# A bound and a masked index list for the last pass of row gathers in a four-layer graph network

## The chip, the cores and the metric

The kernel runs on one core of one Trainium2 chip. The metric is the device time of one execution in microseconds, the median of several runs. A profile is one execution recorded by the hardware profiler; its span runs from the first to the last recorded instruction.

## The reference, cut to what matters

The graph has 6250 nodes of 256 features and 106250 edges, sorted by the node they end in (`dst`). Four layers follow each other. Each normalises the node rows, multiplies them by weights, and sums over each node's incoming edges a weighted copy of the source node's row. In the first layer the weight is a hyperbolic distance factor, in the second and third a softmax-like score, and in the last layer, the one this change is about, there is none:

```python
summed = segment_sum(feat[src], dst, num_segments=n)
deg = segment_sum(ones_like(dst), dst, num_segments=n)
h_neigh = (summed / maximum(deg, 1.0)[:, None]) @ w_neigh.T
rst = feat @ w_self.T + b_self + h_neigh      # x = x + rst
```

## The kernel before, in words

**Tiles and steps.** The 6250 nodes are 49 blocks of 128 (`NB`), the 106250 edges are 831 tiles of 128 (`ET`). Edges are sorted by target, so a tile's edges end in one block, or, where a tile crosses from one block to the next, in two. The work on edges goes in steps. A step is one tile together with one block; a tile that crosses a border is taken twice, once for each block. That gives 831 + 48 = 879 real steps (`S_REAL`), padded to `S` = 880. In `dst_tab` each edge of a step has the number of its target inside the step's block; a number below 0 or above 127 means that the edge belongs to the neighbouring block. `src_tab` holds the source node's number, as an int32. Slots of the last tile and of the last step that hold no edge have source 0 and a target far away.

**A pass over the edges.** Each layer stores its 49 blocks of transformed rows in a table in HBM (6272 rows of 259 float32: 256 features and three extra columns). Then it runs over the 880 steps:

- GpSimd (POOL) gathers, with one indirect DMA for a step, the 128 source rows of the step's edges from the table into a slot of the ring (`ring`, 40 slots, which lies over the tile `X`). In `gathers(q)` (q = 0, 1, 2 for the second to the fourth layer) it waits before every fifth gather until the five slots have been read (semaphore `used`).
- VectorE (DVE) compares 0 to 127 with `dst_tab` and so makes the one-hot matrix of the step. In the last layer `ones` does so for five steps at a time (line 1129). An edge outside the block gets a row of zeros.
- TensorE (PE) multiplies the one-hot matrix with the gathered rows (line 585, `sum_step`). Both blocks' steps of a crossing tile gather the same 128 rows, and the zeros make sure that each edge counts once.
- DVE adds the product to the block's running sum (`add_sum`, line 1142).

**Between the passes** of the third and the fourth layer DVE finishes the last blocks' ELU (`weighed` and `elu`, lines 1670 and 1675) beside ScalarE (ACT, `elu_parts`), then `norm_pipe(3, ...)` adds to X and normalises, PE multiplies by the weights, and SyncE (SP) stores the table. `gathers(2)` begins when all seven parts of the table are stored and X has been saved.

**In the last pass** PE also multiplies each block by `w_self` every 17 steps (lines 560, 567 and 568), and DVE adds `add_mean` (line 1720) in the last 49 steps; then SP stores the result.

**Memory that the change reuses.** `plain` is a scratch tile of 16 x 128 bfloat16 for each partition. In the third pass `dst_rows` lies in it. `not_own` is the tile `w_tab`; the second layer reads it last.

Of the kernel before, what the change touches and what calls it, by code (L numbers as in the profile page):

```python
# [13 lines left out]
P = 128  # L14
F32 = mybir.dt.float32
BF16 = mybir.dt.bfloat16
I32 = mybir.dt.int32
ALU = mybir.AluOpType
# [4 lines left out]
NB = -(-N // P)  # L23
# [9 lines left out]
S = ITERS * RING  # L33
# [8 lines left out]
SLOTS = 40  # L42
# [3 lines left out]
BATCH = 5  # L46
# [30 lines left out]
def gnn_program(nc, x, src, dst, edge_weight, w0, bias0, w1, b1, mag_w, mag_b, attn_w, w2, a2,  # L77
                w_neigh, w_self, b_self, out):
    with ExitStack() as ctx:
        def sb(name, shape, dt=F32):  # L80
            return ctx.enter_context(nc.sbuf_tensor(name, shape, dt))
# [3 lines left out]
        def sem(name):  # L85
            if name not in sems:
                sems[name] = ctx.enter_context(nc.semaphore(name))
            return sems[name]
# [7 lines left out]
        plain = sb("plain", [P, RING, P], BF16)  # L96
        src_tab = sb("src_tab", [P, S], I32)
        dst_tab = sb("dst_tab", [P, S])
# [33 lines left out]
        table = nc.dram_tensor("table", [NB * P, W], F32, kind="Internal").ap()  # L132
# [29 lines left out]
        ring = x_flat[:, 0:SLOTS * W].rearrange("p (k w) -> p k w", k=SLOTS)  # L162
# [19 lines left out]
        hots = onehot[:, 0:HOTS, :]  # L182
        spare = onehot[:, HOTS:, :].rearrange("p k e -> p (k e)")
        plain_flat = plain[:, :, :].rearrange("p k e -> p (k e)")
        dst_rows = plain_flat[:, 0:2 * BATCH * P].rearrange("p (m k e) -> p m k e", m=2, k=BATCH)
        hot_t = spare[:, 0:BATCH * P].bitcast(BF16).rearrange("p (m k e) -> p m k e", m=2, k=BATCH)
        no_link = plain_flat[0:1, 0:CW]
# [5 lines left out]
        not_own = w_tab[:, :]  # L193
# [261 lines left out]
        @block.gpsimd  # L455
        def _(pool):
            pool.iota(iota_i, [[1, S]], base=0, channel_multiplier=0).then_inc(sem("iotas"), 1)
            pool.iota(tno_i, [[P, EC]], base=0, channel_multiplier=1).then_inc(sem("iotas"), 1)
            pool.memset(ident[:, :], 0.0).then_inc(sem("ident_zero"), 1)
            pool.wait_ge(sem("ident_zero"), 1)  # L460
            pool.affine_select(out=ident[:, :], in_=ident[:, :], compare_op=ALU.not_equal, fill=1.0, base=0,
                               pattern=[[-1, P]], channel_multiplier=1).then_inc(sem("iotas"), 1)

            def gathers_layer0():
                for s in range(S):
                    if s % LAND == 0 and s >= SLOTS0:
                        pool.wait_ge(sem("used"), SLOTS + s + LAND - SLOTS0)
                    pool.indirect_dma_start(ring0[:, s % SLOTS0, :], None, table,  # L468
                                            bass.IndirectOffsetOnAxis(src_tab[:, s:s + 1], 0)
                                            ).then_inc(sem(f"batch0_{s // LAND % (SLOTS0 // LAND)}"), 16)  # L470

            def gathers(q):
                pool.wait_ge(sem("x_kept"), 16 * OUTER * (q + 1))
                for s in range(S):
                    if s % BATCH == 0:

                        pool.wait_ge(sem("used"), (q + 1) * S + s + BATCH)
                    pool.indirect_dma_start(ring[:, s % SLOTS, :], None, table,  # L478
                                            bass.IndirectOffsetOnAxis(src_tab[:, s:s + 1], 0)
                                            ).then_inc(sem(f"batch_in{s // BATCH % (SLOTS // BATCH)}"), 16)  # L480

            pool.wait_ge(sem("steps_out"), 16 * (2 * EC + 2))
            pool.memset(A[:, :, :], 0.0).then_inc(sem("sums_zero"), 1)
            pool.wait_ge(sem("table_stored"), 16 * OUTER)
            gathers_layer0()
            for q in range(3):
                pool.wait_ge(sem("table_stored"), 16 * OUTER * (q + 2))
                gathers(q)
# [507 lines left out]
        def _(dve):  # L996
            chain = Chain(dve, "vec_step")
            ts, tt, stt = dve.tensor_scalar, dve.tensor_tensor, dve.scalar_tensor_tensor
# [33 lines left out]
            for c in range(EC):  # L1032
                ins = dve.memset(parts_of["tile"][0][:, c, :], float(P * c))
# [11 lines left out]
            for c in range(EC):  # L1045
                ins = ts(pick[:, c, :], iota_s, t_start[:, c:c + 1], None, ALU.is_ge)
            chain(ins)
            for c in range(EC):
                ins = stt(pick[:, c, :], iota_s, t_end[:, c:c + 1], pick[:, c, :], ALU.is_le, ALU.mult)
            ins.then_inc(sem("tiles_picked"), 1)  # L1050
            dve.wait_ge(sem("weights_turned"), 1)
            for n, name in enumerate(("w0T", "w1T", "wnT", "wsT")):
                ins = dve.tensor_copy(wT[name][:, :, 0:D], psum[:, 4 + n, :].rearrange("p (c d) -> p c d", c=2))
# [9 lines left out]
            for b in range(NB):  # L1063
                ins = dve.bn_stats(out=stats[:, b, 0:6], in_=X[:, b, :])
# [32 lines left out]
            for c in range(EC):  # L1097
                n = min(P, S - c * P)
                ins = dve.tensor_copy(turned_dst[0:n, c, :], psum[0:n, c // 4, c % 4 * P:c % 4 * P + P])
            for h in range(2):  # L1100
                a, z = h * SH, h * SH + SH
                ins = tt(row_b[:, a:z], row_a[:, a:z], dst_tab[0:1, a:z], ALU.subtract)
            chain(ins)
            for h in range(2):
                a, z = h * SH, h * SH + SH
                ins = tt(row_b[:, a:z], row_b[:, a:z], psum[0:1, 2 + h, 0:SH], ALU.add)
# [11 lines left out]
            for c in range(EC):  # L1118
                n = min(P, S - c * P)
                dve.tensor_copy(rows_out[0:n, c, :], turned_dst[0:n, c, :])  # L1120
                ins = tt(cuts_out[0:n, c, 1:P], turned_dst[0:n, c, 1:P], turned_dst[0:n, c, 0:P - 1], ALU.not_equal)
# [50 lines left out]
            def rows(source, k_scale, b):  # L1172
                return ts(blk(source, b), blk(source, b), colb(k_scale, b), None, ALU.mult)
# [491 lines left out]
            def weight_2(b):  # L1665
                dve.reciprocal(col("t1")[:, b:b + 1], A[:, b, AUX:AUX + 1]).then_inc(sem("weights_2"), 1)
# [10 lines left out]
            def scored_sums():  # L1677
                chain(ts(tiny[:, 7:8], iota_part[:, :], float(TAIL), None, ALU.is_ge))
                chain(dve.tensor_copy(iota_psum, iota_node[:, :]))
                for first in range(SUBS):  # L1680
                    turned_hots(0, first)
                equals(1, 0, 0)
                equals(1, 0, CMP)
                leaky_exponents(0, 0)

                def turn(i, last):
                    for h in range(2):
                        at = blocks_at(mybir.EngineType.DVE, i * SLOTS + h * GR, GR)
                        for k in range(GR):
                            add_sum(1, i, h * GR + k, at[k])  # L1690
                            done = i * SLOTS + h * GR + k - ET
                            if 0 <= done < NB - 1:
                                weight_2(done)
                            if done >= 10:
                                weighed(done - 10)
                            if done >= 11:
                                elu(done - 11)
                            if last and h:
                                continue
                            if k in (0, 4, 8, 12):  # L1700
                                turned_hots(i, SUBS + h * SUBS + k // 4)
                            if k == 2:
                                equals(1, i, (h + 1) * GR)
                            if k == 15:
                                leaky_exponents(i, h + 1)
                            if k == 17:
                                equals(1, i, (h + 1) * GR + CMP)

                for i in range(TURNS):
                    turn(i, i == TURNS - 1)  # L1710
                dve.wait_ge(sem("sum_added"), ACC_BANKS + 3 * S)
# [72 lines left out]
            for c in range(OUTER):  # L1784
                if c < BY_DVE:
                    for b in part(c):
                        ins = rows(H, "t1", b)
# [44 lines left out]
            split_u()  # L1832
            scored_sums()

            chain(tt(A[:, NB - 1, AUX:AUX + 1], A[:, NB - 1, AUX:AUX + 1], tiny[:, 7:8], ALU.subtract))
            weight_2(NB - 1)
            dve.wait_ge(sem("weights_2"), NB)
# [39 lines left out]
```

## Time and profile before

| what | value |
|---|---|
| runs of the kernel before (3) | median 5928.48 us, 5926.69 to 5933.43 |
| span of the profiled execution | 5110.8 us |
| median of the runs less that span | 817.7 us |
| instructions recorded | 58785 |
| POOL busy | 3349.8 us (66% of the span) |
| DVE busy | 3431.6 us (67%) |
| PE busy | 3290.4 us (64%) |
| ACT busy | 1841.1 us (36%) |
| last pass's first to last gather | 3991.37 to 5091.0 us |

The profiled execution's own time outside its span is not recorded: of it only the span is known. The 817.7 us are the difference to the runs, and no record of the trace lies in them. In the rows below "PE", "DVE" and so on are engines, L478 is line 478 of the kernel, an arrow points from what an instruction reads to what it writes, and "idle before" is the time for which the engine stood still just ahead of such instructions, with what ended the wait.

### The profile page before, as it was taken

What the parts mean: (1) busy time and instruction counts of PE and PEld (TensorE: products, weight loads), DVE (VectorE), ACT (ScalarE), POOL (GpSimd) and SP (SyncE); (2) the same over time, 40 slices, a digit from 0 to 9 for tenths busy, and PEclk for the clock granted to TensorE, in tenths of its full rate; (3) what the DMA queues carried; (4) which work ended last, traced back from release to release, by engine and by line L of the source; (5) the groups of instructions that cost most, each with busy time, mean ns of one, the idle gap of its engine ahead of it and who ended that gap; (6) DMA issues with size and microseconds to landing.
All of it is one profiled execution on the core that took longest, in us unless ns stands there. A gap on an engine that the chain in (4) does not pass through costs nothing. (4 is left out here: it accounts for less than half of the span.)

```text
span 5110.8 us, 58785 instructions
## 1 busy us (share of the span) xinstructions
PE 3290.4 (64%) x11755; PEld 2256.4 (44%) x11755; DVE 3431.6 (67%) x10603; ACT 1841.1 (36%) x4370; POOL 3349.8 (66%) x3529
## 2 busy tenths in 40 slices
PE   2788888887444655566655666666666666666666
PEld 1556666655332333333334444444444444444444
DVE  7799999999974666666676555555558455555556
ACT  2455555555782333333344333333337100000000
POOL 1777777774007777777752777777772577777776
PEclk7899999998776777777777888888877877778787
DMA  4444444444024333333445554555554444443434
GB/s 137 136 133 132 134 133 133 133 133 120 11 91 124 107 107 107 107 107 107 107 117 153 132 132 132 132 132 134 133 133 141 138 114 114 114 114 107 113 107 142
DMA packets 302511, 617.15 MB, mean 121 GB/s; under 512 B 66649, under 2 KB 175189, under 8 KB 302166
## 3 DMA queue, kind: packets, MB, share of 16 engines
q0 software_dynamic: 168960, 467.01, 34.5%
q1 hardware_dynamic: 107862, 117.55, 7.5%
q10 hardware_dynamic: 25344, 28.85, 2.0%
q8 instruction: 113, 1.85, 0.1%
q14 instruction: 232, 1.90, 0.1%
HBM read 560.58 MB, written 52.57 MB: 120 GB/s over the span
## 5 line engine op out<-in xcount | busy, mean ns | idle before, releaser
L478 POOL DMA_INDIRECT X<-table,src_tab x2640 | 2500.7, 947 | 1360.5 <-issue 752.1
L585 PE MATMUL psum<-X,onehot 128*128 128x259 f32 x5280 | 1847.6, 494 | 905.8 <-ACT onehot L722 333.6
L1142 DVE SCALAR_TENSOR_TENSOR A<-A,same_tab,psum 128x259 f32 x3476 | 1671.8, 481 | 756.9 <-PE psum L585 531.8
L585 PEld LDWEIGHTS psum<-X,onehot 128*128 128x128 f32 x5280 | 1169.2, 241 | 1376.9 <-ACT onehot L722 582.4
L468 POOL DMA_INDIRECT X<-table,src_tab x880 | 836.9, 951 | 280.7 <-issue 251.6
L722 ACT ACTIVATE onehot<-G,zero_col,ecols 128x128 f32<-128x128 bf16 x1760 | 730.0, 481 | 688.9 <-PE psum L585 451.3
L594 PE MATMUL psum<-H,G 128*128 x1760 | 603.1, 429 | 249.6 <-DVE G L1238 196.3
L574 PE MATMUL psum<-X,onehot 128*128 128x259 f32 x1760 | 567.6, 407 | 4.2 <-ACT onehot L722 2.2
L594 PEld LDWEIGHTS psum<-H,G 128*128 128x128 f32 x1760 | 323.7, 205 | 429.0 <-issue 392.1
L722 ACT ACTIVATE onehot<-onehot,zero_col,coef 128x128 f32<-128x128 bf16 x880 | 365.9, 481 | 128.7 <-DVE coef L1281 103.1
L1238 DVE SCALAR_TENSOR_TENSOR G<-psum,X 128x257 f32<-128x257 f32 x880 | 367.1, 418 | 61.8 <-DMA X<-table,src_tab 38.0
L722 ACT ACTIVATE ecols<-ecols,zero_col 128x20 f32<-128x20 f32 (+2 forms) x187 | 52.4, 302 | 987.5 <-DVE ecols L1663 486.9
L574 PEld LDWEIGHTS psum<-X,onehot 128*128 128x128 f32 x1760 | 357.5, 204 | 71.3 <-issue 10.7
L992 ACT COPY onehot<-psum 128x256 f32<-128x256 f32 x49 | 18.2, 372 | 1020.0 <-PE psum L560 1020.0
L1129 DVE TENSOR_TENSOR G<-psum,dst_tab 128x1280 bf16<-128x1280 f32 x176 | 261.3, 1485 | 34.6 <-ACT onehot L722 34.5
L1245 DVE TENSOR_SCALAR onehot<-iota_b,dst_tab 128x128 bf16<-128x128 bf16 x880 | 230.0, 261 | 0.0
L623 PE MATMUL psum<-ident,ecols 128*20 128x128 f32 x44 | 17.0, 387 | 308.5 <-DVE ecols L1539 308.5
L1657 DVE TENSOR_REDUCE ecols<-psum 128x20 f32<-128x60 f32 x44 | 9.7, 221 | 292.0 <-DMA X<-table,src_tab 292.0
L722 ACT ACT_TABLE_LOAD x137 | 175.8, 1283 | 77.5 <-DVE mv L1072 61.3
L1538 DVE TENSOR_TENSOR ecols<-X,w_tab 128x20 f32<-128x20 f32 x44 | 8.2, 186 | 264.3 <-DMA X<-table,src_tab 264.3
L1129 DVE TENSOR_TENSOR onehot<-psum,dst_tab 128x640 f32<-128x640 f32 x176 | 144.1, 819 | 43.6 <-issue 33.4
L616 PE MATMUL psum<-wide_rows,onehot 128*128 x880 | 131.6, 237 | 58.0 <-issue 38.4
(347 smaller groups left out, 2826.0 us busy)
## 6 DMA issues: line engine op xcount, KB each, us to landing
X<-table,src_tab POOLq DMA_INDIRECT x3520, 2.8
plain<-rows_dram SPq DMA_DIRECT2D x110, 256.0 KB
plain<-rows_dram ACTq DMA_DIRECT2D x176, 160.0 KB, 3.4
table<-H SPq DMA_DIRECT2D x21, 906.5 KB, 8.5
x_dram<-X SPq DMA_DIRECT2D x21, 896.0 KB, 4.1
X<-x_dram SPq DMA_DIRECT2D x14, 896.0 KB, 5.1
X<-in_x SPq DMA_DIRECT2D x2, 6144.0 KB
table<-A SPq DMA_DIRECT2D x7, 906.5 KB, 7.2
```

Of the source, the lines that this page charges most:

```text
L468: pool.indirect_dma_start(ring0[:, s % SLOTS0, :], None, table, bass.IndirectOffsetOnAxis(src_tab[:, s:s + 1], 0)).then_inc(sem(f"batch0_{ ...
L478: pool.indirect_dma_start(ring[:, s % SLOTS, :], None, table, bass.IndirectOffsetOnAxis(src_tab[:, s:s + 1], 0)).then_inc(sem(f"batch_in{s ...
L574: pe.matmul(psum[:, s % ACC_BANKS, 0:W], hots0[:, s % HOTS0, :], ring0[:, s % SLOTS0, :], start=True, stop=True).then_inc(sem("used"), 1)
L585: pe.matmul(psum[:, k % ACC_BANKS, 0:W], hots[:, k % HOTS, :], ring[:, k, :], start=True, stop=True).then_inc(sem("used"), 1)
L594: pe.matmul(psum[:, 4 + s % 4, 0:D + 1], oht[:, s // B0 % 2, s % B0, :], blk(H, at, 0, D + 1), start=True, stop=True).then_inc(sem("own_ro ...
L616: ins = pe.matmul(psum[:, 4 + h, c * OWN:c * OWN + P], hot_t[:, first % 2, k, :], u_parts[:, bass.ds(vs[k] * OWN, P)], start=True, stop=True)
L722: return act.activation(out_, in_, f, **kw)
L992: act.copy(late_v, late_turned).then_inc(sem("late_kept"), 1)
L1129: return tt(out_, numbers.rearrange("p (o n) -> p o n", o=1).to_broadcast([P, n, P]), dst_tab[:, bass.ds(first, n)].rearrange("p (s o) -> ...
L1142: stt(total, total, same, psum[:, t % ACC_BANKS, 0:W], ALU.mult, ALU.add).then_inc(sem("sum_added"), 1)
L1238: stt(junk0[:, q, k % 2, at:at + D + 1], psum[:, 4 + s % 4, 0:D + 1], 1.0, ring0[:, s % SLOTS0, 0:D + 1], ALU.mult, ALU.mult, accum_out=en ...
L1245: ts(equal0[:, s % GR0, :], iota_b[:, :], dst_tab[:, s:s + 1], None, ALU.is_equal).then_inc(sem("equal_0"), 1)
```

## The change

The last pass of gathers (q = 2) reads its indices from a new list, `near_tab`, and gets a bound. In `near_tab` each edge that lies in the step's block keeps its source number, and each other one has 2 * 49 * 128 = 12544 added, so that it is above the last row of the table (6271). The gather is issued with `bounds_check` 6271 and `oob_is_err=False`: rows whose index is above the bound are left out, and their places in the ring keep what they held. They are multiplied by zero later, as before. DVE builds the list with four operations after the third layer's sums, and POOL waits for it (semaphore `near`) before the last pass. The second and third layers' gathers are issued as before, and so are the first layer's.

```diff
@@ -182,6 +182,7 @@
         plain_flat = plain[:, :, :].rearrange("p k e -> p (k e)")
+        near_tab = plain[:, :, :].bitcast(I32).rearrange("p k e -> p (k e)")[:, 0:S]
@@ -471,13 +472,20 @@
             def gathers(q):
                 pool.wait_ge(sem("x_kept"), 16 * OUTER * (q + 1))
+                if q == 2:
+                    pool.wait_ge(sem("near"), 1)
                 for s in range(S):
                     if s % BATCH == 0:
                         pool.wait_ge(sem("used"), (q + 1) * S + s + BATCH)
-                    pool.indirect_dma_start(ring[:, s % SLOTS, :], None, table,
-                                            bass.IndirectOffsetOnAxis(src_tab[:, s:s + 1], 0)
-                                            ).then_inc(sem(f"batch_in{s // BATCH % (SLOTS // BATCH)}"), 16)
+                    if q < 2:
+                        ins = pool.indirect_dma_start(ring[:, s % SLOTS, :], None, table,
+                                                      bass.IndirectOffsetOnAxis(src_tab[:, s:s + 1], 0))
+                    else:
+                        ins = pool.indirect_dma_start(ring[:, s % SLOTS, :], None, table,
+                                                      bass.IndirectOffsetOnAxis(near_tab[:, s:s + 1], 0),
+                                                      bounds_check=NB * P - 1, oob_is_err=False)
+                    ins.then_inc(sem(f"batch_in{s // BATCH % (SLOTS // BATCH)}"), 16)
@@ -1832,6 +1840,10 @@
             split_u()
             scored_sums()
+            ts(not_own, dst_tab[:, :], P - 0.5, float(2 * NB * P), ALU.is_gt, ALU.mult)
+            chain(ts(near_tab, dst_tab[:, :], 0.0, float(2 * NB * P), ALU.is_lt, ALU.mult))
+            chain(tt(near_tab, near_tab, not_own, ALU.add))
+            tt(near_tab, near_tab, src_tab[:, :], ALU.add).then_inc(sem("near"), 1)
             chain(tt(A[:, NB - 1, AUX:AUX + 1], A[:, NB - 1, AUX:AUX + 1], tiny[:, 7:8], ALU.subtract))
             weight_2(NB - 1)
```

## Rows read from the trace of the kernel before

**Rows 1.** The page's groups: busy us, mean ns, then idle before and its releaser

```profile
L478 POOL DMA_INDIRECT X<-table,src_tab x2640 | 2500.7, 947 | 1360.5 <-issue 752.1
```

**Rows 2.** The source view of line 478 in the last pass, 3990 to 5111 us

```profile
L478 POOL DMA_INDIRECT X<-table,src_tab x880: 942/946/1165, 3991.4 to 5091.0; - x176
its engine sat idle before it (us, times) until:
  issue: 261.4, 858
  DMA table<-A: 119.2, 1
  PE psum L585: 6.4, 21
who waited for it (us, times):
  PE psum L585: 104.2, 29
DMA to landing us min/median/max: 2.7/2.8/5.5
```

**Rows 3.** The timeline of POOL at the last pass's start: start, us, what, idle before

```profile
3991.37 0.94 POOL L478 DMA_INDIRECT X<-table,src_tab  x1 [119.23 <-DMA table<-A]
3992.62 0.94 POOL L478 DMA_INDIRECT X<-table,src_tab  x1 [0.30 <-issue]
...
4002.63 0.94 POOL L478 DMA_INDIRECT X<-table,src_tab  x1 [0.30 <-issue]
4003.88 0.95 POOL L478 DMA_INDIRECT X<-table,src_tab  x1 [0.30 <-PE psum L585]
4005.13 0.95 POOL L478 DMA_INDIRECT X<-table,src_tab  x1 [0.30 <-issue]
```

**Rows 4.** The windows view of the last pass: length, busy by engine, granted clock, DMA share, GB/s

```profile
3991.00:5092.00 1101.00, 719.02 (x2142) 504.41 (x2142) 577.75 (x1140) 18.23 (x49) 832.83 (x880) 0.78 0.42 115
```

**Rows 5.** The DMA view of the same stretch, and of the whole span (queue 0 carries the gathers)

```profile
q0 software_dynamic: 42165, 116.56, 39.2%
```

```profile
q0 software_dynamic: 168960, 467.01, 34.5%
```

**Rows 6.** The groups view of POOL by shape, and of DVE by shape

```profile
L468 POOL DMA_INDIRECT X<-table,src_tab x880 | 836.9, 951 | 280.7 <-issue 251.6 <-PE psum L574 16.1 <-DMA table<-H 13.0
L461 POOL TENSOR_SCALAR_AFFINE_SELECT ident<-ident 128x128 f32<-128x128 f32 x1 | 0.3, 292 | 0.2 <-POOL ident L459 0.2
L1868 POOL MEMSET const-float32-0.0<- 128x1 f32 x1 | 0.1, 98 | 0.2 <-issue 0.2
```

```profile
L1112 DVE TENSOR_TENSOR H<-H 1x880 f32<-1x880 f32 x1 | 1.1, 1064 | 0.0
L1094 DVE TENSOR_SCALAR A<-A 128x880 f32<-128x880 f32 x1 | 0.6, 619 | 0.1
L1090 DVE CAST misc<-A 1x880 int32<-1x880 f32 x1 | 0.6, 608 | 0.0
```

**Rows 7.** The timeline of DVE behind the third pass's sums

```profile
3907.22 0.16 DVE L1666 RECIPROCAL cols<-A 128x1 f32<-128x1 f32 x1
3907.48 0.18 DVE L1838 MEMSET A<- 128x147 f32 x1
3907.70 0.36 DVE L1670 TENSOR_SCALAR A<-A,cols 128x256 f32<-128x256 f32 x1
3907.97 0.42 DVE L1675 SCALAR_TENSOR_TENSOR A<-H,A 128x256 f32<-128x256 f32 x1
3908.30 0.35 DVE L1670 TENSOR_SCALAR A<-A,cols 128x256 f32<-128x256 f32 x1
...
3915.85 0.75 DVE L1847 TENSOR_TENSOR X<-X,A 128x256 f32<-128x256 f32 x2
```

**Rows 8.** The timeline of ACT there

```profile
3914.09 0.58 ACT L722 ACTIVATE H<-A,zero_col,cols 128x256 f32<-128x256 f32 x1
3914.59 0.89 ACT L722 ACTIVATE H<-H,zero_col 128x256 f32<-128x256 f32 x2
```

**Rows 9.** The chain that ended last, from 4400 to 5092 us, by line

```profile
by line: POOL X L478 59.3%; issue 22.8%; PE psum L585 8.9%; DVE A L1142 3.3%; DMA X<-table,src_tab 1.8%; DVE onehot L1129 1.2%; DVEq L266 0.8%; PE psum L567 0.7%; PE psum L568 0.4%; DVEq L1142 0.4%; DVE H L1720 0.4%; PE psum L560 0.2%; DVE 
```

## The prediction

> **What bounds the kernel now.** I read the page's groups first. They show which instruction stands at the head of the passes: the indirect gathers of line 478, 2640 of them in three passes, 947 ns each [rows 1]. Next comes the last pass by itself, since only its 880 gathers are changed. The source view of line 478 shows that they start from 3991.4 to 5091.0 us, and that POOL stands idle between them for 261.4 + 6.4 us in 879 gaps, put down to its own issuing in 858 of them [rows 2]. The timeline shows the same as a beat: a start every 1.25 us, made of 0.94 or 0.95 us of work and 0.30 us of gap, with no gap longer than another [rows 3]. From first to last start that is (5091.0 - 3991.37) / 879 = 1.251 us, 880 times over 1101 us. POOL is thus never held up by a full ring in this pass: what it does for one gather sets the beat.
>
> The windows view says how much room the others have. In the 1101 us PE is busy 719.0, DVE 577.8, ACT 18.2 and the DMA engines 42% [rows 4]. A step costs PE 0.82 us and DVE 0.66 us against a beat of 1.25. The chain of waits agrees: over most of this stretch 59% is gathers and 23% issue, 9% is the matmuls [rows 9]. PE waits for a gather only 29 times, 104.2 us in all [rows 2]; it takes five steps at a time when they have landed, so such a wait is the beat seen from the other side. The reader is to see two things. A change of the beat goes one for one into the time, 880 times, from a slower beat at once, and from a faster one down to PE's 0.82 us. Bytes moved, PE and DVE work are beside the point in this pass.
>
> The runs' median, 5928.5 us, is 817.7 us above the profiled span, 5110.8. No row lies in that difference. I take it as unchanged and add the change of the span to the median.
>
> **How many rows are left out.** 880 steps of 128 are 112640 places. Each of the 106250 edges is in its step's block exactly once. So 6390 places, 5.7%, get an index above the bound: 48 crossing tiles taken twice give 48 x 128 = 6144, the last tile's empty places 118, the padded step 128. They lie in some 98 steps; in the other 782, 89%, every row is gathered as before. That weighs on all that follows: whatever the bound costs is paid 880 times, and what it saves is saved in one gather of nine.
>
> **The change part by part.**
>
> *The wait for `near`.* It is an extra wait at the head of the pass. POOL stands there anyway from the third pass's last gather until the table is stored, 119.23 us [rows 3]; the list is ready near 3911, some 80 us before 3991.37. It costs nothing. Without that cover it would cost what is left of the four operations, under 4 us.
>
> *The four DVE operations.* Two TENSOR_SCALAR over 128 x 880: 619 ns for float32, and writing int32 the nearest row is the CAST at 608 ns. Two TENSOR_TENSOR at 1064 ns, the row of 880 float32 [rows 6]. The sum is 2 x 0.62 + 2 x 1.06 = 3.4 us. They stand ahead of `weight_2` of the last block, which starts at 3907.22, and what is queued behind them on DVE is the last ten blocks' ELU and then `norm_pipe(3)`, whose start, at 3915.85, sets the table store and so the first gather. But DVE isn't what sets the pace of these ten blocks at their end: it begins with 0.60 us for a block (3907.70 to 3908.30) and ends waiting for ACT, whose last exponential runs to 3915.48 [rows 7, 8]. ACT isn't late by it: it needs `weight_2` of the last block, now near 3910.8, for the Relu at 3914.09. Ten blocks at 0.60 from 3911.1 end at 3917.1, where they ended at 3915.85: +1.3 us. Bounds: 0 if the operations overlap more, 3.4 if none of it is taken up. I take 1.4, which all goes into the fill between the passes.
>
> *The bytes.* 6390 rows of 1036 bytes are 6.6 MB of the 116.6 MB that queue 0 moves there [rows 5]. The transfers take 2.8 us from issue to landing and forty slots are in flight ahead of PE [rows 2], so a slightly shorter transfer moves nothing. What I take: 0. Semaphore counts are the same, sixteen for each gather, so nothing waits otherwise.
>
> *The register with the bound.* Each gather now carries a bound, perhaps with an instruction of POOL's queue to set it. The nearest row is the semaphore wait that already stands ahead of every fifth gather: the gap with it is 0.30 us as is the one without [rows 3]. POOL's queue takes such an instruction for nothing, while the gather before it works. I take 0; if it lay in the gap, even 30 ns would be 26 us, and that is counted with the next part.
>
> *The gather itself.* No row of this trace has a gather with a bound, so it is bounded from both sides. Work of a gather is 0.946 us for 128 rows, 7.4 ns a row, if none of it is fixed [rows 2]. Below: rows left out cost nothing and the test is free, then the pass is shorter by 6390 x 7.4 ns = 47 us. Above: the test is a piece of work by itself. POOL's smallest instruction, one element in each of 128 partitions, takes 98 ns; its compare-and-select over 128 x 128 takes 292 ns [rows 6]. A list of 128 indices is one element for each row, so the first is nearer. 880 x 0.098 = 86 us; the other, 880 x 0.292 = 257 us. Between -47 and +86 (far end +257) I take 0: nothing in the rows shows that POOL's time follows anything but the count of gathers. The first layer's 880 gathers write to another ring, with other waits, and take 951 ns against 947 [rows 1, 6].
>
> Here the Trainium skill speaks, in "DMA: Bandwidth & Descriptors". Its section "Anatomy of one DMA" has descriptor generation as a small variable share and says that many descriptors can be emitted before the added cost shows: by this rule a gather with fewer rows is no shorter on POOL, and the sum would be 1.4 us instead of down to -46. Its section "SWDGE vs HWDGE vs iDMA" has these DMAs made by software that computes the descriptors, on a core of GpSimd: by that, one more comparison for each index can cost time, which speaks against the change. No row here has two sizes of gather to decide between them.
>
> **The sum.** 0 (wait) + 1.4 (DVE) + 0 (bytes) + 0 (register) + 0 (gather) = +1.4 us on the span of 5110.8, and 5928.5 + 1.4 = 5930 us on the median.
>
> **The rivals.** Of 5928.5 us 0.2% is 11.9 us; that is about what a measurement can tell from no change.
>
> *Nothing to see (0.40).* The bounded gather keeps its 0.946 us and its 0.30 us gap. For it: the regularity of both under different rings and waits. 5930, and 5917 to 5940 with a few ns either way on each gather.
>
> *The test costs time on POOL (0.36).* It is the one on the slower side. The place is the work of each gather, 0.946 us; the price is 0.098 us for each, 6016 us with the DVE term. It decides from (11.9 - 1.4) / 880 = 12 ns for a gather, a tenth of a ns for each index. For it: it is paid 880 times by the one engine without slack, and software that handles 128 indices in 0.946 us has no compare that is known to be free. Against it: the unbounded gather may test already, and skip nothing.
>
> *Rows left out shorten the gather (0.24).* All of the work follows the rows and the test is free: 5930 - 47 = 5883 us. If half of 0.946 us is fixed, -24 gives 5906. It decides from -13.3 us, or 28% of the work following the rows. For it: the descriptors of 128 rows are the obvious thing to take 0.946 us. Against it: it can happen only in one gather of nine, and any test of over 0.3 ns for an index would eat it whole.
>
> *A rival that changes neither sum:* less traffic would let PE run nearer its own pace. DMA engines are at 42% and PE at 65% of the stretch [rows 4], so it is hidden anyway, and I count it with the first.
>
> **How the numbers follow.** Likeliest: 5930. The low end is the third case in full, 5883. The high end takes in the second case at its nearer bound, 6016, with 4 us for the DVE bound and the runs' spread: 6020. Above it stays what a test nearer to the 292 ns row would make, up to 6187, to which I give 0.12, and below 5883 next to nothing. The likeliest case's own range is 5917 to 5940. Faster by over 0.2%: 0.24; within: 0.40; slower: 0.36.
>
> **What would show it right or wrong.** In the profile after, the source view of the bounded gather in the last pass: median 946 ns and a start every 1.25 us for the first case; near 1040 ns or a gap above 0.30 us in all 880 for the second; for the third a low minimum in about 98 gathers, those at block borders, and the old 946 in the rest. The last pass's first gather should start 1 to 2 us later than 3991.4, and DVE should show four operations of 3.4 us in all ahead of `weight_2`. Queue 0 should move some 6.6 MB less. The prediction is wrong if the beat of the pass moves by more than 12 ns.

## The result, and the profile after

| | median us | runs |
|---|---|---|
| before | 5927.35 | 20, 5918.19 to 5935.75 |
| changed | 5937.6 | 20, 5928.73 to 5951.26 |

The ratio is 1.0019, 95% interval 1.0013 to 1.0025: 11 us slower by the ratio, 10 by the medians, just inside the 11.9 us that count as no change here. Two later sets of runs gave 1.0022, just outside it. The forecast of 5930 in a range of 5883 to 6020 holds, but not by the way it was argued: the bound is not free, and most of its price didn't reach the end.

The first surprise is the page of the changed kernel. Its span is 5937.8 us, as long as its runs. That of the kernel before was 5110.8, 818 us short of them.

```profile
span 5937.8 us, 59670 instructions
PE 3574.5 (60%) x11755; PEld 2297.5 (39%) x11755; DVE 3424.2 (58%) x10607; ACT 1855.8 (31%) x4370; POOL 3391.0 (57%) x3529
PE 17%; issue 10%; another core or an unknown queue 10%; DVE 8%; ACT 2%; DVEq 2%; DMA 0%; ACTq 0%; POOL 0%; POOLq 0%
```

The last of these lines is the chain that ended last over the whole span. POOL has 0% in it, but that proves little: the shares add up to about half of the span, and in the run with the bound alone, told below, where POOL's beat explains the whole cost, POOL has 1%. DVE works as long as before, POOL 41 us more, and PE 284 us more for the same 11755 matmuls (3290.4 before). The rest of the 827 us between the two spans is waits.

The source view of the bounded gathers (line 485 now) in the changed kernel answers to [rows 2], and the groups of its page to [rows 1]:

```profile
L485 POOLq MOVE  x880: 29/29/29, 4609.7 to 5881.7; - x176
L485 POOL DMA_INDIRECT X<-table,plain x880: 992/998/1271, 4610.4 to 5892.7; - x176
  issue: 238.1, 781
  DMA table<-A: 135.8, 1
  PE psum L593: 103.1, 77
  remote: 63.8, 21
```

```profile
L482 POOL DMA_INDIRECT X<-table,src_tab x1760 | 1663.9, 945 | 1347.9 <-issue 494.2
L485 POOL DMA_INDIRECT X<-table,plain x880 | 878.2, 998 | 540.8 <-issue 238.1
```

Three things are to be read. The bounded gather takes 998 ns against 946 [rows 2], while the unbounded ones of the same execution keep 945. A register MOVE of 29 ns for the bound stands in POOL's queue before each. And the pass isn't on POOL's beat: 98 gaps, 166.9 us in all, end with something other than POOL's own issuing. 46 gaps are longer than 1 us, 149.0 us together, and each of them stands ahead of a fifth gather, where POOL waits for five ring slots. The pass takes 1282 us from first to last gather; 880 gathers at their beat of 1.303 would take 1146. ("remote" is a releaser that the trace doesn't hold; it sits at the same kind of place as the waits put down to PE.)

Queue 0 of the whole span, which answers to the second of [rows 5], and the stretch of the last pass, which answers to [rows 4]:

```profile
q0 software_dynamic: 168960, 460.41, 29.2%
```

```profile
4610.00:5893.00 1283.00, 763.89 (x2098) 443.53 (x2098) 545.60 (x1082) 18.23 (x49) 877.56 (x880) 0.70 0.34 92
```

The bytes fall by 6.6 MB, as worked out, and the count of packets not at all: the rows left out still have their packets' places. A few per cent of PE's and DVE's records are missing in this stretch.

The four new operations, in DVE's timeline; the last is recorded as a custom instruction on 16-bit halves, and the four take 3.4 us in all as forecast:

```profile
4524.88 0.61 DVE L1843 TENSOR_SCALAR w_tab<-dst_tab 128x880 f32<-128x880 f32 x1
4525.41 0.61 DVE L1844 TENSOR_SCALAR plain<-dst_tab 128x880 int32<-128x880 f32 x1
4526.05 1.08 DVE L1845 TENSOR_TENSOR plain<-plain,w_tab 128x880 int32<-128x880 int32 x1
4527.16 1.08 DVE L1846 CUSTOM_DVE_ANT_0 plain<-plain,src_tab 128x1760 uint16<-128x1760 uint16 x1
```

### The profile page after: what moved, and what is told of

The parts are those of the page before. It is cut to its first block and busy times, and to the rows that moved or that the text cites. A ratio compares the mean times of both kernels' runs of the same rounds, so it can differ in the third digit from the quotient of the medians.

```text
span 5937.8 us, 59670 instructions
## 1 busy us (share of the span) xinstructions
PE 3574.5 (60%) x11755; PEld 2297.5 (39%) x11755; DVE 3424.2 (58%) x10607; ACT 1855.8 (31%) x4370; POOL 3391.0 (57%) x3529
## 3 DMA queue, kind: packets, MB, share of 16 engines
q0 software_dynamic: 168960, 460.41, 29.2%
## 5 line engine op out<-in xcount | busy, mean ns | idle before, releaser
L593 PE MATMUL psum<-X,onehot 128*128 128x259 f32 x5280 | 2059.6, 525 | 1320.5 <-DVE A L1150 991.3
L482 POOL DMA_INDIRECT X<-table,src_tab x1760 | 1663.9, 945 | 1347.9 <-issue 494.2
L593 PEld LDWEIGHTS psum<-X,onehot 128*128 128x128 f32 x5280 | 1169.1, 249 | 1986.0 <-issue 1046.3
L485 POOL DMA_INDIRECT X<-table,plain x880 | 878.2, 998 | 540.8 <-issue 238.1
L469 POOL DMA_INDIRECT X<-table,src_tab x880 | 836.6, 951 | 512.5 <-issue 244.4
L602 PE MATMUL psum<-H,G 128*128 x1760 | 645.5, 454 | 417.6 <-DVE G L1246 225.8
L582 PE MATMUL psum<-X,onehot 128*128 128x259 f32 x1760 | 596.0, 425 | 4.1 <-DVE A L1150 3.1
L602 PEld LDWEIGHTS psum<-H,G 128*128 128x128 f32 x1760 | 341.6, 217 | 623.0 <-issue 582.0
L582 PEld LDWEIGHTS psum<-X,onehot 128*128 128x128 f32 x1760 | 377.8, 216 | 80.6 <-issue 9.6
L1253 DVE TENSOR_SCALAR onehot<-iota_b,dst_tab 128x128 bf16<-128x128 bf16 x880 | 242.4, 275 | 0.0
L757 ACT CAST G<-G 128x1024 f32<-128x1024 bf16 x110 | 114.0, 1037 | 217.5 <-remote 114.7
L624 PEld LDWEIGHTS psum<-wide_rows,onehot 128*128 128x128 bf16 x880 | 86.8, 102 | 168.1 <-issue 144.1
```

Of the source, the lines that this page charges most:

```text
L482: ins = pool.indirect_dma_start(ring[:, s % SLOTS, :], None, table, bass.IndirectOffsetOnAxis(src_tab[:, s:s + 1], 0))
L485: ins = pool.indirect_dma_start(ring[:, s % SLOTS, :], None, table, bass.IndirectOffsetOnAxis(near_tab[:, s:s + 1], 0), bounds_check=NB * ...
L582: pe.matmul(psum[:, s % ACC_BANKS, 0:W], hots0[:, s % HOTS0, :], ring0[:, s % SLOTS0, :], start=True, stop=True).then_inc(sem("used"), 1)
L593: pe.matmul(psum[:, k % ACC_BANKS, 0:W], hots[:, k % HOTS, :], ring[:, k, :], start=True, stop=True).then_inc(sem("used"), 1)
L602: pe.matmul(psum[:, 4 + s % 4, 0:D + 1], oht[:, s // B0 % 2, s % B0, :], blk(H, at, 0, D + 1), start=True, stop=True).then_inc(sem("own_ro ...
L624: ins = pe.matmul(psum[:, 4 + h, c * OWN:c * OWN + P], hot_t[:, first % 2, k, :], u_parts[:, bass.ds(vs[k] * OWN, P)], start=True, stop=True)
```

## The experiments

The kernel before came out at two levels: 5109 and 5121 us in two sets of runs, 5934 and 5936 in two others, and 5927 in the first timing. Within a set it was the same for all kernels, so each run is compared with the runs of before in its own set. I name them the low and the high level. The first profile of before is of the low level, its timed runs are of the high one. The two low sets ran on chips 3 and 5, the two high ones on chips 6 and 4; for the first timing the chip is not on record. So level, chip and set go together here and can't be told apart.

**The kernel before, again.** No edit.

> The kernel before, unchanged, profiled and timed anew. The profile of the changed kernel has a span of 5937.8 us, close to its runs; the profile of before had 5110.8 us against runs of 5928. Theory A (the first profile of before was an execution unlike the timed ones, in which PE and DVE handed work to each other without long waits): the time is within 0.1% of before, the profile's span is near 5926 us, the last pass takes about 1270 us and not 1101, and POOL waits for a full ring in it. Theory B (profiling of before simply leaves 818 us out, and the timed runs have the same 1.25 us beat): the span is 5111 us again, POOL waits for nothing.

Measured at the low level: 5110.76 us, ratio 1.0002 (0.9993 to 1.0011), span 5108.6. The source view of the last pass:

```profile
L478 POOL DMA_INDIRECT X<-table,src_tab x880: 942/946/1276, 3988.5 to 5088.6; - x176
  issue: 259.2, 851
```

Neither theory as put. The first profile is faithful, to executions of this level; span and time agree within some 2 us here; and the 818 us are the distance of the two levels. Theory A was right that the timed executions were another kind, wrong in taking the profiled one for an exception: all 11 runs came out like it here.

**The bound alone**, in the last pass (diff shortened).

```diff
-  pool.indirect_dma_start(ring[...], None, table, IndirectOffsetOnAxis(src_tab[:, s:s + 1], 0)
+  bound = dict(bounds_check=NB * P - 1, oob_is_err=False) if q == 2 else {}
+  pool.indirect_dma_start(ring[...], None, table, IndirectOffsetOnAxis(src_tab[:, s:s + 1], 0), **bound
```

> The last pass's gathers get the bound 6271 but keep the old index list, so no row is left out; no list is built. Theory A (the bound adds 52 ns to each gather, most of it hidden because POOL has slack in the pass): gathers of 998 ns, start to start 1.30 us where nothing holds them, and 5 to 12 us (0.1 to 0.2%) on the time. Rival (POOL's beat sets the pass, and the rows left out gave 36 us back in the changed kernel): 880 x 0.052 = 46 us, 0.8%. Rival (the bound is free, the list and its new address cost the time): 946 ns and no change.

Measured at the low level: 5157.3 us against 5109.4, ratio 1.0090 (1.0076 to 1.0104), +48 us. The source view of its last pass:

```profile
L479 POOLq MOVE  x880: 29/29/29, 3990.0 to 5120.5; - x176
L479 POOL DMA_INDIRECT X<-table,src_tab x880: 994/998/1277, 3990.7 to 5136.7; - x176
  issue: 230.5, 756
  PE psum L586: 37.5, 123
DMA to landing us min/median/max: 2.7/2.8/5.6
```

The pass grows from 1100.1 to 1145.9 us: 880 x 52 ns. No row is left out here and the gather has the same 998 ns as in the changed kernel, so the price belongs to the bound. At this level the rival with POOL's beat is right and theory A's "hidden" is not. The mean gap stays what it was, (230.5 + 37.5) / 879 = 0.305 us, so the MOVE costs POOL nothing. Its queue runs ahead: the last MOVE is at 5120.5 us, 16 us before the last gather.

**The list alone.** The changed kernel with its last pass gathering from the old list without a bound:

```diff
-  bass.IndirectOffsetOnAxis(near_tab[:, s:s + 1], 0), bounds_check=NB * P - 1, oob_is_err=False)
+  bass.IndirectOffsetOnAxis(src_tab[:, s:s + 1], 0))
```

> The four DVE operations and the wait for the list as in the change, but the last pass gathers from the old list without a bound, so no row is left out. Theory A: 0 to 3 us (under 0.05%), from 3.4 us of DVE work of which some is taken up behind ACT. Rival (the list is the cost): about 10 us, 0.17%.

Measured at the low level: 5110.45 against 5109.4, ratio 1.0004 (0.9995 to 1.0013). The pass takes 1100.2 us, and its first gather starts at 3987.9 us, against 3988.5 in the kernel before. The list costs nothing that can be seen in the time. DVE's timeline shows where part of it went; the first line is the first of the last blocks' ELU, the second the start of `norm_pipe(3)`, and both answer to [rows 7]:

```profile
3906.84 0.35 DVE L1677 TENSOR_SCALAR A<-A,cols 128x256 f32<-128x256 f32 x1
3913.16 0.75 DVE L1858 TENSOR_TENSOR X<-X,A 128x256 f32<-128x256 f32 x2
```

The stretch takes 6.3 us, and took 8.15 before (3907.70 to 3915.85): 1.8 of the list's 3.4 us are taken up there, and 1.6 are left, too little to show in the time.

**The bound on three passes.** As the bound alone, without `if q == 2`.

> The bound on the gathers of three passes (second to fourth layer), old index list everywhere, so no row is left out. It triples the suspected cost. Theory A (52 ns a gather, partly hidden behind PE, DVE and ACT in each pass): 15 to 35 us, 0.25 to 0.6%, far from 137. Rival (POOL's beat sets all three passes): 2640 x 0.052 = 137 us, 2.3%. Rival (the bound is free): no change.

Measured at the low level: 5248.88, ratio 1.0274 (1.0260 to 1.0288), +139.5 us; 137 were worked out for POOL's beat in all three. Nothing of it is hidden at this level.

**The changed kernel, twice more.** No edit.

> The changed kernel, unchanged. In the first timing both kernels took about 5930 us; in the runs since, the kernel before takes 5109 us, and the bound alone cost 48 us. Theory A (POOL's beat sets the pass when a pass takes 1101 us, and is partly hidden when it takes 1283): if before is at 5109 here, the change costs 44 to 52 us, 0.9 to 1.0%; if before is at 5927 again, 7 to 14 us. Rival (the rows left out give time back, which the bound alone cannot show): clearly under 40 us where before is at 5109.

> The changed kernel once more. The same kernel before has taken 5109 us in one set of runs and 5934 in another, so the level of this set is not known ahead. Theory A (52 ns on each gather; all of it counts where POOL's beat sets the pass, most is taken out of POOL's waits for the ring where it doesn't): with before at 5109, 44 to 52 us more, 5153 to 5161 us, the last pass 880 x 1.303 = 1147 us long. With before at 5934, 8 to 16 us more. Rival (rows left out give back part of it at the faster level): at 5109, less than the 48 us of the bound alone by 10 us or more.

Both fell on the high level. 5945.52 against 5933.65, ratio 1.0022 (1.0013 to 1.0032); 5950.2 against 5935.71, ratio 1.0022 (1.0012 to 1.0031). So +12 to +14 us, as expected for that level. The changed kernel as a whole has not been timed at the low level; the runs with the bound alone and the list alone add up to 49 us there (47.9 and 1.05).

**The kernel before at the high level.**

> The kernel before, for its profile beside the changed one on the same chip. Theory A, if the level is 5934: gathers of 946 ns, start to start 1.25 us where nothing holds them, a last pass of about 1270 us, and POOL's waits for the ring 25 to 40 us longer in all than the changed kernel's 136. If the level is 5109: as the first profile, POOL never held up.

One run, 5941.58 us. The source view of its last pass:

```profile
L478 POOL DMA_INDIRECT X<-table,src_tab x880: 941/949/1092, 4619.2 to 5889.2; - x176
  issue: 244.8, 801
  DMA table<-A: 133.8, 1
  remote: 106.9, 32
  PE psum L585: 85.0, 46
```

This is the comparison that the first profile couldn't give. Before: 1270.0 us from first to last gather, with 78 gaps that POOL didn't make itself, 191.9 us. Changed: 1282.2 us, 98 gaps, 166.9 us. The work of the gathers grew from 835 to 878 us (949 and 998 ns), 43 us; the gaps of all kinds, without the wait for the table, fell from 436.7 to 405.0, 32 us. What is left is 11 to 12 us, as much as the loss in the medians. The last passes of the two later profiles of the changed kernel are as long, 1282.1 and 1281.8 us. The whole spans of single executions don't carry this: the one of before is 5939.6, the three of the changed kernel 5937.8, 5943.9 and 5963.8.

The timelines of POOL show how the gaps give it back. First before, then changed (its second profile), both at the high level:

```profile
5008.13 0.94 POOL L478 DMA_INDIRECT X<-table,src_tab  x1 [4.97 <-PE psum L585]
5009.38 0.95 POOL L478 DMA_INDIRECT X<-table,src_tab  x1 [0.30 <-issue]
...
5025.68 0.95 POOL L478 DMA_INDIRECT X<-table,src_tab  x1 [0.30 <-issue]
5029.65 0.94 POOL L478 DMA_INDIRECT X<-table,src_tab  x1 [3.02 <-PE psum L585]
```

```profile
5213.06 0.99 POOL L485 DMA_INDIRECT X<-table,plain  x1 [3.56 <-PE psum L593]
5214.36 1.00 POOL L485 DMA_INDIRECT X<-table,plain  x1 [0.30 <-issue]
...
5237.80 1.00 POOL L485 DMA_INDIRECT X<-table,plain  x1 [0.30 <-issue]
5242.34 0.99 POOL L485 DMA_INDIRECT X<-table,plain  x1 [3.54 <-remote]
```

Here POOL does 15 gathers at its beat before and waits 3 us; changed, it does 20 and waits 3.5. These are the commonest stretches: before, 29 of 52 long waits follow 15 gathers and 17 follow 20; in the first profile of the changed kernel 8 of 46 follow 15 and 32 follow 20. In the whole pass, waits of over 1 us are 52 with 184.0 us before, and 46 with 149.0 in the first profile of the changed kernel (46 with 148.5 and 44 with 145.4 in the two others). Of the 46 us that 880 bounds cost, 35 to 39 come back from these waits. Most of that is their number, 52 against 44 to 46; they are also somewhat shorter, 3.2 to 3.3 us in the mean against 3.5.

**More rows left out.** The changed kernel with the indices of partitions 64 to 127 all above the bound:

```diff
-  tt(near_tab, near_tab, src_tab[:, :], ALU.add).then_inc(sem("near"), 1)
+  chain(tt(near_tab, near_tab, src_tab[:, :], ALU.add))
+  ts(near_tab[64:P, :], dst_tab[64:P, :], 0.0, float(2 * NB * P), ALU.mult, ALU.add).then_inc(sem("near"), 1)
```

> As the change, but in all 880 steps of the last pass the list sends the 64 indices of partitions 64 to 127 above the bound, so 56320 rows more are left out and the last layer's sums lack those edges. Theory A (POOL's work for a gather doesn't follow the rows left out): gathers of 998 ns, time within 0.2% of the changed kernel. Rival (it follows them): at 7.4 ns for a row up to 0.47 us less for each gather, until PE's 0.84 us a step sets the pass; 200 us and more below the changed kernel. Queue 0 moves some 60 MB less in both.

Measured at the high level: 5956.01 against 5933.65, ratio 1.0035 (1.0023 to 1.0048), where the changed kernel had 1.0022 in the same set. The source view, queue 0 of the whole span, and the last pass in the windows view:

```profile
L485 POOL DMA_INDIRECT X<-table,plain x880: 992/998/1285, 4625.1 to 5909.6; - x176
```

```profile
q0 software_dynamic: 168960, 405.59, 26.1%
```

```profile
4620.00:5900.00 1280.00, 760.33 (x2074) 441.45 (x2075) 535.53 (x1056) 18.26 (x49) 870.20 (x872) 0.69 0.19 49
```

The gather has the same 998 ns with over half of its rows left out; the DMA share falls from 34% to 19% and nothing gets faster. The rival, rows left out shorten the gather, is refuted, and no gain from less traffic shows at this level. The run is even 10 us slower than the changed kernel; its one further DVE operation is too short to explain that, and the cause is not shown.

**Fewer rows without a bound.** The kernel before with gathers of 64 rows in the last pass (shortened):

```diff
-  pool.indirect_dma_start(ring[:, s % SLOTS, :], None, table, IndirectOffsetOnAxis(src_tab[:, s:s + 1], 0)
+  n = 64 if q == 2 else P
+  pool.indirect_dma_start(ring[0:n, s % SLOTS, :], None, table, IndirectOffsetOnAxis(src_tab[0:n, s:s + 1], 0)
```

> No bound and no list, but each gather of the last pass takes 64 rows, for partitions 0 to 63; the other 64 rows of each slot keep what they held, so the last layer's sums are not those of the graph. It asks what POOL's time for a gather follows. Theory A (rows left out by a bound save nothing, since POOL still goes through all 128 indices): with 64 indices in the list the gather is clearly shorter than 946 ns, 500 to 800. Rival (POOL's time for a gather is a fixed one): 946 ns. On the time: with a beat under 1.1 us at the level of 5109 a pass of 880 x 0.82 to 1.1, 130 us and more less; at the level of 5934, where POOL waits for the ring, less than half of that.

Measured at the low level: 5078.85 against 5120.94, ratio 0.9915 (0.9899 to 0.9932), 42 us less. The source view:

```profile
L479 POOL DMA_INDIRECT X<-table,src_tab x880: 893/900/1170, 4001.3 to 5061.8; - x176
```

Both sides missed: the expected 500 to 800 ns were far too low, and a wholly fixed time is wrong too. 64 rows fewer save 46 ns, 0.7 ns a row; some 854 of the 946 ns don't follow the rows, if the line through the two points is extended. The saving, 880 x 46 ns = 40 us, reaches the end whole. My estimate from this slope: even a bound that spared POOL every row left out could win at most 6390 x 0.72 ns = 4.6 us.

**The bound with an error in place of leaving out.** As the bound alone, without `oob_is_err=False`.

> The last pass's gathers with the bound 6271, old list, but with an index above it counted as an error instead of left out. Theory A1 (the 52 ns come with the bound itself, whatever is to be done with a row above it): gathers of 998 ns, and the time as with the bound and left-out rows: 48 us over before if that is at 5109, 8 to 16 us if it is at 5934. Rival A2 (they come with leaving rows out): 946 ns and no change.

Measured at the low level: 5178.04 against 5120.94, ratio 1.0113 (1.0096 to 1.0129), +57 us. The source view:

```profile
L479 POOL DMA_INDIRECT X<-table,src_tab x880: 1007/1012/1275, 3995.4 to 5153.3; - x176
```

1012 ns, 66 more than without a bound and 14 more than when rows are left out; 880 x 66 ns = 58 us. The price comes with the bound, whichever way it is used: A1, with a size that it had too small. Here too no index was above the bound.

**A slower DVE, without and with the bound.**

```diff
   add_sum(2, i, t, at[t % GR])
+  dve.wait_ge(sem("idled"), i * SLOTS + t)
+  dve.memset(not_own[:, 0:700], 0.0).then_inc(sem("idled"), 1)
```

> The kernel before with one more DVE instruction in each step of the last pass, a memset of 128 x 700 float32 to a tile that is no longer read, about 0.75 us, so that DVE needs about 1.4 us a step and is slower than POOL's 1.25. Expected by both theories: the pass takes about 880 x 1.4 = 1230 us, 100 to 150 us over before, with POOL waiting for a full ring. It is the base for the next run.

> The same with the bound on the last pass's gathers, old list, no row left out. Theory A (the 52 ns are hidden where another engine sets the pass): within 5 us of the kernel with the slow DVE and no bound, while the gathers take 998 ns. Rival (the bound costs time in another way than by POOL's beat, for instance in transfers or in PE's waits): 40 to 50 us over it, as without the slow DVE.

Measured at the high level: 5960.55 (ratio 1.0041, 1.0028 to 1.0054) and, with the bound, 5999.59 (1.0110, 1.0095 to 1.0124). Both expectations fell. The first allowed 100 to 150 us and got 27. The memset took 642 ns instead of 750 and the adds 406 instead of 483, so a step cost DVE about 1.22 us (0.642 + 0.406 + 0.779 / 5 for `ones` + 0.02 for the blocks' own rows) and DVE never became slower than POOL's 1.25. The last pass came out no longer (1267.7 us of gathers). In the profiled execution, the slowest of its five, what was added stands around the pass: the first gather starts 11 us later than in the profile of the kernel before (of the other high set), and 74.5 us follow the last one's start, where 50.4 did. The second said that the bound would vanish; it cost 39 us, about its rival's 40 to 50. Since DVE had not come to set the pass, that isn't a clean test of the rule; it does show that waits for the ring, 185 us of them, need not hide a cost. The source views of the last pass, without and with the bound:

```profile
L478 POOL DMA_INDIRECT X<-table,src_tab x880: 940/946/1669, 4630.3 to 5898.1; - x176
```

```profile
L479 POOL DMA_INDIRECT X<-table,src_tab x880: 992/998/1430, 4618.8 to 5924.9; - x176
```

1267.7 and 1306.0 us. Waits of over 1 us: 63 with 184.9 us, and 52 with 174.5. Here they give back 10 of 46 us, where in the kernels without the memset they give back 35 or more. So at the high level the refund is not the same for two kernels that differ only in DVE's work; what sets it is not shown. "POOL has slack, so its cost is hidden" describes the outcome of the change, and isn't a rule by which one could have computed it.

## Why the prediction came out right, and where its argument failed

*By its own signs.* It called itself wrong if the beat of the pass moved by more than 12 ns. The beat moved by 52 ns: from 1.251 to 1.304 us from start to start in the run with the bound alone. The gather of 998 ns in all 880 steps is the sign named for the second case, the test on POOL, to which it gave 0.36, and not for the first, "nothing to see", from which the 5930 came. That the time still fell between 5917 and 5940 is luck.

*What bounds the kernel.* "POOL is never held up by a full ring in this pass" holds at the low level, where every gather that gets longer or shorter shows in full (+48, +139.5, +57 and -42 us against 46, 137, 58 and 40 worked out). It fails for the executions that the forecast was about. The first step that broke is the sentence on the 817.7 us, "I take it as unchanged and add the change of the span to the median". It was the sign that the profile was of another kind of execution. The four passes of 880 gathers take 1326.5, 1281.4, 1289.9 and 1270.1 us from first to last start at the high level against 1103.7, 1098.9, 1102.2 and 1099.6 in the first profile: 764 of the 829 us between the spans lie in the passes whose beat I had taken from the trace.

*The gather itself, taken as 0.* The second step that broke: it is 52 ns, against a bound of 98 from the nearest row. The reason for the 0, that nothing in the rows shows POOL's time following anything but the count of gathers, was no evidence for a bound, since no row had one. This was the second rival's mechanism ("the test costs time on POOL"), at half its price, and it would have made the kernel slower by 46 us, 0.8 to 0.9%, had the timing been at the level of the profile. The case decides from 12 ns by that rival's own working, so the forecast of no change would have been wrong there.

*The lower bound, 7.4 ns a row.* Ten times too large. The slope is 0.72 ns without a bound, and 0 with one. The rule weighed there from the Trainium skill ("DMA: Bandwidth & Descriptors", section "Anatomy of one DMA"), that many descriptors can be emitted before the cost shows, agrees with the trace: 64 of them cost 46 ns of 946.

*The register, 0.* Right: a MOVE of 29 ns, hidden behind the gathers ahead of it, with the gap at 0.305 us.

*The list, 3.4 us of DVE and 1.4 on the end.* The sum is 3.4; on the end it is 1 us by the medians of the list alone (5110.45 against 5109.4) and inside the interval of no change. The first gather there starts no later, where 1 to 2 us were expected. By DVE's timeline 1.8 us are taken up behind ACT, as argued, and 1.6 are left, against the 1.4 of the forecast.

*The bytes, 0, and the wait for `near`, 0.* Right. 6.6 MB less were moved; half of all rows left out brought nothing, though that was run at the high level alone.

*The sum.* +1.4 us was forecast, about +11 measured. The terms are 46 for the bound, about 1 for the list, and some -35 from fewer waits for the ring. Two errors, each larger than the result, nearly cancelled: a price left at nothing, and a slack not seen. That they did so is luck.

**What stays open.** Why the kernel has two levels. POOL's and DVE's instructions take the same time at both (946 and 949 ns for a gather, DVE busy 3431.6 us in the first profile and 3421.6 at the high level). PE's don't, over the whole span: it is busy 3290.4 and 3551.9 us, with a mean granted clock of 0.81 and 0.75. Its largest group, from the groups view, first at the low level, then at the high one:

```profile
L585 PE MATMUL psum<-X,onehot 128*128 128x259 f32 x5280 | 1847.6, 494 | 905.8 <-ACT onehot L722 333.6 <-DVE A L1142 188.6 <-issue 144.0
L585 PE MATMUL psum<-X,onehot 128*128 128x259 f32 x5280 | 2068.2, 530 | 1313.1 <-DVE A L1142 994.6 <-issue 248.5 <-ACT onehot L722 49.4
```

The larger part is waits between PE and DVE inside the passes: PE's for DVE's adds grow from 188.6 to 994.6 us. Whether the lower clock makes the waits or the waits the lower clock is not shown, nor what part the chip has. In the last pass PE is busy alike, 719.0 and 720.8 us, though 54 of its records fewer are there at the high level. The waits view of the kernel before at the high level, 4620 to 5880 us (total us, times, longest), has DVE's adds waiting 397.9 us in the last pass for something that the trace doesn't name:

```profile
PE psum L585 <- DVE A L1142: 448.4, 164, 12.0
DVE A L1142 <- remote: 397.9, 89, 13.6
```

PE in turn waits 448.4 us for those adds. Traces of the kernel before and the changed one at the high level hold 25646 to 25909 semaphore updates and those of before at the low level 81638 and 81648, so much of what released whom can't be read there. No kernel here could choose its level, so the cause wasn't tried. Nor is it shown what sets the 15 or 20 gathers between two waits; they are multiples of the five slots for which POOL waits at once.

## What to carry to other kernels

Before a beat is read from a profile, hold its span against the timed runs: where they differ by more than the change is worth, every term priced "one for one on the path" needs a second price for executions that wait elsewhere. Where the issuing engine sets the pace, masking indices to skip rows pays only if its work follows the rows; measure the gather with half its rows first, which costs one run. And when an engine works in bursts against a ring, slack doesn't say what lengthening its work will cost: here 46 us of work cost 10 to 14 in one kernel and 39 in another. The count of its waits, and not only their length, changes.

## What the runs showed of the hardware

An indirect gather of rows of 1036 bytes takes POOL 946 ns for 128 rows and 900 for 64. A bound adds 52 ns when rows above it are to be left out, whether or not any row is above it, and 66 when they are to be errors, run with no row above it. Leaving 64 and more of the 128 rows out changes neither the 998 ns nor the number of packets (168960 in all), only the bytes. Start to start, a gather takes 0.305 us more than its duration in the last passes read at the low level, and the MOVE of 29 ns that sets a bound's register adds nothing to it. The same program ran at 5109 us and at 5934 us in different sets of runs, on different chips, with a mean granted TensorE clock of 0.81 and 0.75.
